# Three mixtures of experts in two token streams, with the other stream's norm, convolution and routing placed between the units

## The reference

```
x = x + _L0_conv_ref(_ln_c(x), ...)      # 3x3 convolutions and an attention over pixels
t = t + _L0_ffn_ref(_ln_t(t), ...)       # experts chosen by Sinkhorn and top-k
x = x + _L1_conv_ref(_ln_c(x), ...)      # 7x7 filter made from the image itself
t = t + _L1_ffn_ref(_ln_t(t), ...)       # mixture: 8 experts, 512 hidden, Silu, top 2
x = x + _L2_conv_ref(_ln_c(x), ...)      # a gate from pooled channels at shifted positions
t = t + _L2_ffn_ref(_ln_t(t), ...)       # mixture: 8 experts, 512 hidden, Gelu, top 2
x = x + _L3_conv_ref(_ln_c(x), ...)      # 1 - wf * sigmoid(scale * saliency)
t = t + _L3_ffn_ref(_ln_t(t), ...)       # mixture: 8 experts, 256 hidden, Relu, top 2
```

## Time and profile before

| | |
|---|---|
| median of 3 runs | 446.46 us (445.94 to 451.52) |
| profiled execution | 449.38 us |
| its span | 447.6 us |
| mean granted clock of TensorE | 0.958 of full speed |
| busy: TensorE, its weight loads | 411.0, 290.4 us |
| busy: VectorE, ScalarE, GpSimd | 250.2, 268.8, 155.5 us |
| transfers | 28.74 MB, mean 64 GB/s; 24 loads of spread scores of 512 KB, 3.7 us each |

### The profile page before, as it was taken

The page is one execution under the profiler, slowest core; times in us unless marked ns, Lnnn a source line. Parts: engine busy times, 40 slices in busy tenths (PEclk is TensorE's granted clock), DMA queues, the critical chain, the costliest instruction groups (busy, mean ns, idle before and its releaser), DMA issues.

```text
span 447.6 us, 5042 instructions
## 1 busy us (share of the span) xinstructions
PE 411.0 (92%) x1677; PEld 290.4 (65%) x1677; DVE 250.2 (56%) x524; ACT 268.8 (60%) x496; POOL 155.5 (35%) x151
## 2 busy tenths in 40 slices
PE   7899988887899988999999998899999999898995
PEld 2467647543645566888888654578888885376884
DVE  1624215795433447666566673856666666566776
ACT  5112133693210485777777647678888886777993
POOL 3900000195100011655554600135555532015773
PEclk9969996999889989999999999889999999989999
DMA  8920000005400003111115000041111100005221
GB/s 265 437 98 0 0 0 2 1 0 189 187 0 1 1 0 108 70 42 53 54 49 196 0 1 0 4 143 46 47 48 47 49 1 0 0 4 183 90 92 60
DMA packets 7153, 28.74 MB, mean 64 GB/s; under 512 B 655, under 2 KB 1807, under 8 KB 6872
## 3 DMA queue, kind: packets, MB, share of 16 engines
q1 hardware_dynamic: 7128, 28.43, 17.5%
HBM read 27.81 MB, written 0.62 MB: 64 GB/s over the span
## 4 chain that ended last, share of the span: by engine, by line
PE 66%; DVE 16%; ACT 10%; DMA 3%; issue 2%; POOL 1%; SPq 0%; ACTq 0%; DVEq 0%
PE ps L375 17%; PE ps L377 16%; PE ps L376 16%; PE ps L382 2%; PE ps L606 2%; PE ps L552 2%; ACT hidh L839 2%; DMA w<-in_w_bottom 2%; PE ps L387 2%; ACT rstd L739 2%; ACT rstd L741 2%; ACT ps L840 2%; DVE xn L923 1%; PE ps L435 1%; DVE bot L1016 1%
## 5 line engine op out<-in xcount | busy, mean ns | idle before, releaser
L1100 DVE TENSOR_TENSOR hidl<-ps,hidh 128x512 fp32r<-128x512 f32 x160 | 109.7, 690 | 80.9 <-ACT ps L840 80.9
L359 POOL TENSOR_TENSOR x<-x,rstd 128x512 f32<-128x512 f32 x42 | 54.1, 1292 | 93.4 <-DVE rstd L1162 46.0
L839 ACT ACTIVATE hidh<-ps,par 128x512 fp32r<-128x512 f32 x96 | 67.3, 702 | 23.5 <-PE ps L377 22.9
L375 PE MATMUL ps<-xh,wst_h 128*128 128x512 f32 x160 | 66.4, 415 | 7.3 <-DVE hidl L1100 7.2
L375 PE MATMUL ps<-hidh,wst_h 128*128 128x512 f32 (+1 forms) x170 | 65.2, 383 | 2.2 <-DVE hidl L1100 2.2
L377 PE MATMUL ps<-xl,wst_h 128*128 128x512 f32 x160 | 65.8, 411 | 0.0
L376 PE MATMUL ps<-xh,wst_l 128*128 128x512 f32 x160 | 65.6, 410 | 0.0
L840 ACT ACTIVATE ps<-ps,par 128x512 f32<-128x512 f32 x96 | 64.8, 675 | 0.0
L377 PE MATMUL ps<-hidl,wst_h 128*128 128x512 f32 (+1 forms) x170 | 64.3, 378 | 0.0
L376 PE MATMUL ps<-hidh,wst_l 128*128 128x512 f32 (+1 forms) x170 | 64.2, 377 | 0.0
L839 ACT ACTIVATE hidh<-ps 128x512 fp32r<-128x512 f32 x64 | 38.5, 602 | 23.8 <-PE ps L377 23.8
(11 more groups left out here) (225 smaller groups left out, 615.1 us busy)
## 6 DMA issues: line engine op xcount, KB each, us to landing
scores_all<-rows_scratch SPq DMA_DIRECT2D x24, 512.0 KB, 3.7
wa<-in_moe SPq DMA_DIRECT2D x1, 4096.0 KB, 19.3
wb<-in_moe SPq DMA_DIRECT2D x1, 4096.0 KB, 12.2
wa<-in_moe SPq DMA_DIRECT2D x1, 2048.0 KB, 8.7
dft_x<-in_dft_x SPq DMA_DIRECT2D x1, 640.0 KB
dft_o<-in_dft_o SPq DMA_DIRECT2D x1, 640.0 KB
w<-in_w_bottom SPq DMA_DIRECT2D x1, 576.0 KB, 7.7
w<-in_w_out SPq DMA_DIRECT2D x1, 576.0 KB, 9.4
```

Source lines behind the costliest of these rows:

```text
L359: pool.tensor_tensor(half(x, h), half(x, h), half(parts, h), ALU.add).then_inc(s["state_added"], 1)
L375: pe.matmul(o, wh, xhi, start=start, stop=False)
L839: act.activation(hidh[:, h, f, :], sums, func, bias=bias).then_inc(s["hidden_hi_act"], 1)
L1100: dve.tensor_tensor(hidl[:, h, f, :], bank(h % (4 // q_n) * q_n + f), f32(hidh[:, h, f, :]), ALU.subtract).then_inc(s["hidden_lo"], 1)
```

## The change

From the norm ahead of the first mixture on, the two halves become two streams. The 48 units are numbered through: block `kb` = 2 x mixture + half has 8 units, one for each expert, so the blocks are mixture 1 half 0, mixture 1 half 1, mixture 2 half 0, and so on. While a block of one half runs, the other half's steps are put, one by one, between the units in every engine's queue: in blocks 1 and 2 norm 4, the gate and norm 5 with the routing; in blocks 3 and 4 norm 6, the saliency and norm 7 with the routing. The routing of the first mixture's halves stands between the chunks of the first units. No `keep_clock` is left there but five products after norm 3.

With it come:
- `wst_h`, `wst_l` become `wh_all`, `wl_all`, which hold all eight experts of a mixture split; `wb` ends with the first layers, and every mixture is loaded into `wa`. GpSimd splits all of the first mixture before it adds anything, the second in block 1 (an expert after each unit) and the third in block 3.
- Exp and Sigmoid of routing, gate and saliency are written as Tanh, which is in the sets of Silu and of Gelu: the routing's Exp(z) is (1+t)/(1-t) with t = Tanh(z/2). Ln and Exp of the norms still need their own set, so each inverse root has a load ahead and a load behind.
- Routing works on 4 tiles (half the tokens), and its softmax of the second mixture takes the largest from the logits.
- The scores are spread for one unit at a time (256 KB) into four slots; `parts` has its own buffer; in the last block sums rotate over four banks of PSUM.
- Sums of the front have one set of four banks in the wide units; norms, logits, offsets and turns use banks 6 and 7.
- The last unit's output leaves in two pieces.

TensorE's order (new code, the blocks 1 and 2; those behind are built alike):

```diff
+            norm(3)
+            keep_clock(5, 0)
+            logits(0)
+            front(0)
+            logits(1)
+
+            for n in range(E):
+                front(n + 1)
+                back(n)
+                if n == 0:
+                    turn_route(0)
+                elif n == 3:
+                    turn_route(1)
+
+            for kb in (1, 2):
+                nx = kb + 1
+                hh = nx % 2
+                for j in range(E):
+                    front(kb * E + j + 1)
+                    if j == 0:
+                        center(4, hh)
+                    elif j == 4:
+                        deform(hh)
+                    elif j == 5:
+                        variance(5, hh)
+                    elif j == 6:
+                        logits(nx)
+                    elif j == 7:
+                        turn_route(nx)
+                    back(kb * E + j)
+                    if j == 0:
+                        variance(4, hh)
+                    elif j == 2:
+                        offsets(hh)
+                    elif j == 4:
+                        center(5, hh)
...
+            def turn_route(kb):
...
+                pe.wait_ge(s["routed"], kb + 1)
...
+            def front(n):
...
+                if h == 0:
+                    pe.wait_ge(s["w_split"], kb // 2 * E + e + 1)
+                wh, wl = wh_all[:, n % E, :], wl_all[:, n % E, :]
+                for f in range(q_n):
+                    wait_count(pe, "hidden_lo", sums_free(n, f))
```

ScalarE's and VectorE's order in the same blocks, and VectorE's routing:

```diff
+                for j in range(1, E + 1):
+                    for f in range(4):
+                        hidden(kb * E + j, f)
+                        if (j, f) == (1, 3):
+                            square(4, hh)
+                        elif (j, f) in ((2, 3), (6, 3)):
+                            act.preload_act_table_set("natural_log_exp_and_others")
+                            inverse_root(4 if j == 2 else 5, hh)
+                            act.preload_act_table_set(own)
+                            if j == 6:
+                                high_part(5, hh)
+                        elif (j, f) == (4, 3):
+                            hats(hh)
+                        elif (j, f) == (5, 2):
+                            gate_tanh(hh)
+                        elif (j, f) == (6, 0):
+                            square(5, hh)
+                        elif (j, f) == (7, 3):
+                            route_tanh(kb + 1)
+                            act.preload_act_table_set("gelu_and_others")
...
+                for j in range(1, E + 1):
+                    n = kb * E + j
+                    for f in range(4):
+                        low(n, f)
+                        if (j, f) == (5, 2):
+                            gate_half(hh)
+                        elif (j, f) == (8, 2):
+                            keep_rows(kb + 1)
+                    scale(n - 1)
+                    if j == 2:
+                        offset_inputs(hh)
+                    elif j == 3:
+                        positions(hh)
+                    elif j == 6:
+                        norm_half(5, hh)
+                        norm_low(5, hh, 4 + kb + 2)
+                        route_start(kb + 1)
+                        route_pick(kb + 1)
+                    elif j == 7:
+                        route_end(kb + 1)
...
+            def route_end(kb):
+
+                m, h = divmod(kb, 2)
+                dve.wait_ge(s["exp_out"], kb + 1)
+                step(dve.tensor_scalar(seg(rem, h), seg(ew, h), -1.0, 1.0, ALU.mult, ALU.add))
+                step(dve.reciprocal(seg(oh2, h), seg(rem, h)))
+                step(dve.scalar_tensor_tensor(seg(ew, h), seg(ew, h), 1.0, seg(oh2, h), ALU.add, ALU.mult))
+                if MOE[m]["layer"] == 2:
+
+                    step(dve.tensor_reduce(quad(r8, h), tiles(seg(ew, h)), AX.X, ALU.add))
+                    step(dve.reciprocal(quad(r8b, h), quad(r8, h)))
+                    step(dve.tensor_tensor(tiles(seg(ew, h)), tiles(seg(ew, h)), over(quad(r8b, h), E), ALU.mult))
+                step(dve.scalar_tensor_tensor(seg(wgt, h), seg(oh1, h), BIG, seg(ew, h), ALU.is_equal, ALU.mult))
+                step(dve.tensor_reduce(quad(r8, h), tiles(seg(wgt, h)), AX.X, ALU.add))
+                if MOE[m]["layer"] == 2:
+                    step(dve.tensor_scalar(quad(r8, h), quad(r8, h), 1e-6, None, ALU.add))
+                step(dve.reciprocal(quad(r8b, h), quad(r8, h)))
+                dve.tensor_tensor(tiles(seg(wgt, h)), tiles(seg(wgt, h)), over(quad(r8b, h), E), ALU.mult).then_inc(s["routed"], 1)
```

GpSimd's order, and SyncE's reload of `wa`:

```diff
+            def split_expert(e, w):
+                pool.tensor_copy(wh_all[:, e, 0:w], wa[:, e, 0:w])
+                pool.drain()
+                for first in range(0, w, 512):
+                    cols = slice(first, first + 512)
+                    last = pool.tensor_tensor(wl_all[:, e, cols], wa[:, e, cols], f32(wh_all[:, e, cols]), ALU.subtract)
+                last.then_inc(s["w_split"], 1)
...
+            x_ready(pool, 2, 1)
+            pool.wait_ge(s["moe1_loaded"], 16)
+            for e in range(E):
+                split_expert(e, 1024)
+            for n in range(E):
+                add_part(n)
+            pool.wait_ge(s["moe2_loaded"], 16)
+            for n in range(E, 2 * E):
+                add_part(n)
+                pool.wait_ge(s["part_sums"], n + 1)
+                split_expert(n % E, 1024)
+            for n in range(2 * E, 3 * E):
+                add_part(n)
+            for n in range(3 * E, 4 * E):
+                add_part(n)
+                pool.wait_ge(s["moe3_loaded"], 16)
+                split_expert(n % E, 512)
+            for n in range(4 * E, UNITS - 1):
+                add_part(n)
...
-            sp.wait_ge(s["x2_ready"], 2)
-            sp.dma_start(wb[:], dram["moe2"]).then_inc(s["moe2_loaded"], 16)
+            sp.wait_ge(s["w_split"], E)
+            sp.dma_start(wa[:], dram["moe2"]).then_inc(s["moe2_loaded"], 16)
```

More of the change, by code:

```diff
@@ L720, in _, with logits @@
-            keep_clock(4, 7)
-            mixture(2)
+            def logits(kb):
+                m, h = divmod(kb, 2)
+                pe.wait_ge(s["normed"], seq(MOE[m]["ln"], h))
+                if kb == 1:
+                    pe.wait_ge(s["exp_in"], 1)
+                for t in range(4):
+                    last = pe.matmul(bank(7, cols=E, first=t * E), half(xn, h)[:, t * C:(t + 1) * C], p(MOE[m]["router"]),
+                                     start=True, stop=True)
+                last.then_inc(s["logits_done"], 1)
@@ new lines, in _ @@
+            for j in range(E):
+                front(3 * E + j + 1)
+                if j == 0:
+                    center(6, 0)
+                elif j == 4:
+                    center(7, 0)
+                elif j == 5:
+                    variance(7, 0)
+                elif j == 6:
+                    logits(4)
+                elif j == 7:
+                    turn_route(4)
+                back(3 * E + j)
+                if j == 0:
+                    variance(6, 0)
+                elif j == 2:
+                    saliency(0)
@@ new lines, in _ @@
+            for j in range(E):
+                front(4 * E + j + 1)
+                if j == 1:
+                    variance(6, 1)
+                elif j == 4:
+                    variance(7, 1)
+                back(4 * E + j)
+                if j == 0:
+                    center(6, 1)
+                elif j == 2:
+                    saliency(1)
+                elif j == 3:
+                    center(7, 1)
+                elif j == 5:
+                    logits(5)
+            for j in range(E - 1):
+                front(5 * E + j + 1)
+                if j == 0:
+                    turn_route(5)
+                back(5 * E + j)
@@ L886, in _ @@
[L886 to L894 removed]
+                bias = p(spec["b1"])[:, e * q_n + f:e * q_n + f + 1] if spec["b1"] else 0.0
@@ L897, in _ @@
+            for n in range(5 * E + 1, UNITS):
+                for f in range(2):
+                    hidden(n, f)
         @block.vector
@@ new lines, in _ @@
+            for j in range(1, E + 1):
+                n = 4 * E + j
+                for f in range(2):
+                    low(n, f)
+                    if (j, f) == (4, 0):
+                        saliency_half(1)
+                scale(n - 1)
+                if j == 2:
+                    saliency_inputs(1)
+                elif j == 3:
+                    threshold(1)
+                elif j == 5:
+                    norm_half(7, 1)
+                    norm_low(7, 1, 4 + 6)
+                elif j == 6:
+                    route_start(5)
+                    route_pick(5)
+                elif j == 7:
+                    route_end(5)
@@ L1258, in constants @@
+            low(5 * E + 1, 0)
+            low(5 * E + 1, 1)
+            keep_rows(5)
+            for n in range(5 * E + 2, UNITS):
+                for f in range(2):
+                    low(n, f)
```

(3 more changed lines are left out.)

784 lines of the change are left out of this document (395 added, 389 removed).

## The result

The changed kernel took 456.44 us (median of 4 runs, 454.66 to 459.37) beside 447.25 for the kernel before: ratio 1.0221, 95% interval 1.0171 to 1.0272. On a second chip it took 454.56 beside 446.02: 1.0161 (1.0087 to 1.0235). Ratios leave out executions more than 1.5% longer than the fastest of their kernel, medians and ranges do not. So the changed kernel takes longer, clear of the spread, but both intervals contain 1.02: on which side of 2% it lies stays open. The forecast was 452 with "within 2%" the likeliest class; its span, 453.2, was met by the profiled execution: 452.9 in 454.66 us, the shortest of the four.

The account below looks back on a forecast made before the run. TensorE bounds the mixtures, chains of norm, convolution and routing the gaps. Span 415.0 without waits, plus 17.5 order, 17.5 GpSimd collisions and 3.2 clock gave 453.2, scaled to 452 us; range 434 to 464.

Parts of the forecast that it names:

- The number: Last step, from span to time: span 453.2 us, lowered by the 0.65% the profiled execution exceeded its median, gives 452.
- Clock: TensorE's granted clock falling to 1.2 GHz after waits: two falls charged, at the start and in block 1, 3.2 us.
- my case: The prediction's main case for the whole kernel: 452 us, range 444 to 458, chance 0.46.
- the prediction's own sign: Test stated beforehand for the slower-clock alternative: granted clock near 0.5 in more than three stretches.
- the clock takes it: Rival: eight TensorE waits, from the filter stage to block 5, each cost 1.6 us of clock; 462 us, chance 0.25.
- VectorE behind GpSimd: VectorE's small steps wait for GpSimd's running instruction, in the filter stage and blocks 1 to 5: 17.5 us.
- The rival of little cost: GpSimd's work hardly delays VectorE's steps, which slip into its gaps: 434.5 us, chance 0.24.
- Waits of the order: Waits the instruction order itself makes in blocks 0 to 5, sharpest at turn_route: 17.5 us.
- Tail: Time after the last product: 4.4 us, with at most some tenths gained by sending output in smaller pieces.
- Table loads: ScalarE's activation table loads: 19 after 148.4 where 6 were, each charged 1.28 us without added drain.
- 470: Rival: ScalarE is held 1.3 us longer at each table load, 19 us in all; time 470 us, chance 0.03.
- The sum without waits: TensorE's work from first front to tail with no wait: span 415.0 us, 33 under the 447.6 before.

## Why the prediction was right or wrong

**The step that failed is "The number"**, the way from the span to the time, and behind it the term "Clock", which charged two falls where the profile shows four. Its 0.65% was a property of one execution: the kernel before, over 13 runs on the second chip, had spans of 442.4 to 450.7 at mean granted clocks of 0.969 to 0.954, and its profiled one (447.6, 0.958) was a long one, while the changed kernel's (452.9, 0.950) was the shortest of four on the first chip and a middle one on the second. Subtracting 0.65% made 452 out of 453.2, where the span and the 1.8 us that lie around it (455.0) would have been the better forecast of its median of 454.6 to 456.4. Of the 4.4 us between 452 and 456.4 this step makes 3.0; the other 1.4 is that the executions behind the first median are longer than the sum. It also put my case, and with it "within 2%", further from the bound of 455.4 than the sum had it.

**Clock.** Charged: two falls, 3.2 us. The profile has four in the mixtures: at the start, behind the turns of blocks 1 and 3, and behind center(7, 1). What each costs, with and without it: 1.6 at the start (1.05 given back in block 0), 1.3 to 1.6 in block 1, 1.6 in block 3; and block 4 took 34.1 with a fall and 32.6 without. So 3.4 to 5.2 us in the mixtures, and more in the filter stage, for which nothing was charged (13.7 us at 1.2 GHz, 6.8 in the kernel before). By the ratios, filling every wait was worth 3 us, by the medians 5.5. By the prediction's own sign, more than three stretches near 0.5, the rival "the clock takes it" has its condition met, and the first median lies above its 455.4; but 8 falls and 462 were too many: behind equal waits the clock sometimes stays. (The sum says four falls decide; two more than charged make 455.2, just short of 455.4.)

**VectorE behind GpSimd.** Right in mechanism. Block 1: 7.2 forecast; without its splits it is 6.1 to 6.4 shorter, of which 1.3 to 1.6 is the clock's fall behind the longer wait (59.9 where that wait is filled, 55.1 without the splits). Block 3: 2.0, measured 1.3. The filter stage was charged 5.0 and gave 8.7 to 9.2 when the splits were held, since the stretch at 1.2 GHz went with the delays; against the kernel before it grew by 5.3 to 5.8, because that kernel loses 4.0 there itself, which the sum had not seen. The rival of little cost (434.5) is refuted. One reading of the trace of before was too strong: that no such instruction ran through under GpSimd's. At 373.41 VectorE's x<-x,rstd of 128x256 started 3 ns ahead of GpSimd's subtraction and took its usual 0.42, and the subtraction took 1.01 where its like take 0.73 to 0.75. It is the one that starts second that waits; so too at 249.82, where 1.29 is usual:

```profile
249.42 0.80 DVE L1188 TENSOR_TENSOR x<-x,rstd 128x512 f32<-128x512 f32 x1
249.82 1.56 POOL L335 TENSOR_TENSOR wst_l<-wb,wst_h 128x512 fp32r<-128x512 f32 x1
```

**Waits of the order.** turn_route: 2.2, 2.6, 3.3 forecast without collisions, 2.56, 2.90 and 3.74 measured without splits; with them 4.34 in block 1 where 6.6 was forecast. I had the chain of collisions with add, cast and both subtractions, but made it cost 2.3 us more than it did.

**Tail.** 4.4 forecast, 6.4 measured: a term carried over from before without looking at what it ends in. The last step now waits for GpSimd's last two adds:

```profile
445.88 2.62 POOL L367 TENSOR_TENSOR x<-x,parts 128x512 f32<-128x512 f32 x2 [1.50 <-DVE parts L1226]
...
448.59 0.48 DVE L1353 SCALAR_TENSOR_TENSOR parts<-ps,par,scores_all 128x256 f32<-128x256 f32 x1 [2.19 <-POOL x L367]
```

**Table loads.** 19 of 1.28 us as charged, and none held ScalarE longer, so 470 is out:

```profile
254.28 1.28 ACT L959 ACT_TABLE_LOAD   x1
255.57 0.63 ACT L825 ACTIVATE xh<-xn 128x512 fp32r<-128x512 f32 x1
```

The Trainium skill (ScalarE: Activation LUTs, What ACT_TABLE_LOAD costs) would have about 1.38 us of drain in that gap of 0.01; the measurement decides against it here.

The span came out within 0.3 us because the errors cancelled: blocks 3, 4, 5 and the tail took 5.6 more than their rows, the stretch to front(9) and blocks 1 and 2 took 2.8 less, and the 3.2 of clock were already in them. That agreement is not evidence for each term; the experiments are.

**Where the gain went.** The sum without waits was 33 us under the span of before. What came back: 5 to 6 us in the filter stage, 6 to collisions in blocks 1 and 3 (4.8 and 1.3, worked out from one profile of each kernel), 9.2 to turn_route's waits that remain without splits, 3 to 5 to the clock, 2 to the tail; the remaining 10 or so are the smaller waits, for low parts above all, and were not taken apart. Edits of order and 8 fillers, with no work taken away, recover 23 to 24 us (454.6 to 430.3 and 431.6).

## What to carry to other kernels

When work is moved to overlap, look first at what it now runs beside: VectorE's small steps between SBUF tiles (tensor_scalar, tensor_tensor and scalar_tensor_tensor here, not reciprocals and reductions) take as long as what is left of the GpSimd instruction they meet, so GpSimd's bulk work belongs where VectorE reads PSUM, and the trigger of a GpSimd step (here scale) belongs behind the chain that must be quick. Put the short chain that TensorE waits for first in the queue of its engine, and TensorE's own independent work ahead of the wait. Compare a forecast of a span with spans of many executions and their clocks, not with the ratio of one execution to the median.

## What was unexpected of the hardware

- Behind the same wait of 2.9 us at block 2's turn the granted clock stayed at 1.00 in some profiles and went to 0.59 to 0.61 over 7.4 us in others, which costs 2.7 us, with the same order in the blocks too. Behind the wait of 2.17 us at front(0) and that of 2.35 at center(7, 1) it varied as well; behind the wait of 4.34 in block 1 it fell in every profile that has it. What decides it stays open.
- Filling a wait of 3 us with products did not keep the clock in the execution profiled: it fell 3 us after the last of them, behind waits of 0.59 and 0.84 us and small products. Where every wait from the filter stage on was filled, it fell once more, behind the one that then opened.
- A 128x512 subtraction of two SBUF tiles on VectorE takes 0.68 to 0.69 us beside an idle GpSimd and took 1.54 beside its subtractions:

```profile
256.23 1.54 DVE L1048 TENSOR_TENSOR xl<-xn,xh 128x512 fp32r<-128x512 f32 x1 [1.25 <-ACT xh L825]
```
